# The parts of q and k: from SBUF straight into the stacks, instead of by a copy in DRAM

## What is computed

```
xn  = layernorm(x)
q,k,v = split(xn @ w_in.T + b_in)          # 16 heads of 8 features
scores = q @ k.T / sqrt(8), only where |i - j| <= 128
x1  = x + (xn + softmax(scores) @ v @ w_out.T + b_out) + int8_matmul(xn)
```

## Time and profile before

| | |
|---|---|
| median of 3 runs | 575.05 us (573.01 to 579.34) |
| the profiled execution | 578.81 us, its span 577.1 us |
| busy: PE, DVE, ACT, POOL | 87%, 76%, 59%, 53% of the span |
| mean granted clock of TensorE | 0.936 of full speed |
| DMA | 60.99 MB, 106 GB/s over the span |

### The profile page before, as it was taken

How to read it: one execution, slowest core, us unless ns; L and a number is a source line. 1 busy time by engine, 2 the same in 40 slices (tenths; PEclk the granted TensorE clock), 3 DMA queues, 4 the chain that set the end, 5 groups by cost and what they waited for, 6 DMA issues and landing times. The chain is left out here.

```text
span 577.1 us, 17179 instructions
## 1 busy us (share of the span) xinstructions
PE 499.8 (87%) x5731; PEld 320.9 (56%) x5731; DVE 440.9 (76%) x1888; ACT 341.7 (59%) x867; POOL 305.0 (53%) x361
## 2 busy tenths in 40 slices
PE   6278999999988998999989998988976899999990
PEld 5124444444443443444434446666654899999990
DVE  6698889798898896898886724899979567666662
ACT  2071777776766776577755675756556155555550
POOL 5680844816645556358110020557777567777662
PEclk9575999999999997999998999999998899999996
DMA  3856146274481653553810020711112233455534
GB/s 80 206 130 127 42 122 140 75 163 100 123 155 47 160 111 94 128 100 106 154 56 23 19 75 25 292 37 39 44 51 80 75 99 103 130 171 169 154 89 132
DMA packets 51383, 60.99 MB, mean 106 GB/s; under 512 B 10002, under 2 KB 42134, under 8 KB 49697
## 3 DMA queue, kind: packets, MB, share of 16 engines
q1 hardware_dynamic: 45824, 50.26, 36.0%
q0 software_dynamic: 4320, 8.47, 4.3%
q10 hardware_dynamic: 1152, 1.18, 0.7%
HBM read 31.68 MB, written 28.39 MB: 104 GB/s over the span
## 5 line engine op out<-in xcount | busy, mean ns | idle before, releaser
L704 DVE CUSTOM_DVE_ANT_0 A<-A,band 128x320 f32<-128x320 f32 (+2 forms) x512 | 213.6, 465 | 42.4 <-PE A L881 41.2
L881 PE MATMUL A<-Ks,Qs 48*64 48x320 bf16 (+2 forms) x1024 | 133.1, 310 | 22.5 <-DVE mneg L704 16.5
L911 PE MATMUL SB<-Qs,Ks 50*64 50x320 bf16 (+2 forms) x1024 | 133.8, 299 | 1.3 <-issue 0.6
L557 ACT ACTIVATE Pb<-SB 128x320 f32<-128x320 f32 x256 | 98.5, 441 | 42.2 <-PE SB L925 40.9
L881 PEld LDWEIGHTS A<-Ks,Qs 48*64 48x64 bf16 x1024 | 49.0, 107 | 128.1 <-DVE mneg L704 102.8
L1807 POOL DMA_INDIRECT results<-y,xt x71 | 73.9, 1041 | 36.1 <-issue 25.5
L554 ACT ACTIVATE Pb<-SB 128x384 f32<-128x384 f32 (+1 forms) x128 | 66.4, 545 | 43.8 <-PE SB L925 43.4
L938 PE MATMUL PV<-Pb,Va 128*32 128x320 f32 (+2 forms) x1024 | 87.5, 414 | 1.9 <-ACT Pb L554 1.6
L1258 POOL DMA_INDIRECT expert_rows<-pay,pos x64 | 61.9, 968 | 49.5 <-DVE pay L1441 30.9
L925 PE MATMUL SB<-ends,ident 64*64 64x128 bf16 x768 | 84.7, 222 | 0.0
L1928 PE MATMUL l_S<-xT,wt 128*128 128x128 f32 x568 | 75.1, 275 | 0.0
(11 more groups left out here) (264 smaller groups left out, 859.4 us busy)
## 6 DMA issues: line engine op xcount, KB each, us to landing
Qs<-parts_dram SPq DMA_DIRECT2D x14, 384.0 KB, 5.7
Ks<-parts_dram SPq DMA_DIRECT2D x14, 384.0 KB, 9.7
xt<-expert_rows SPq DMA_DIRECT2D x71, 65.0 KB, 1.9
yb<-results SPq DMA_DIRECT2D x7, 512.0 KB, 4.2
parts_dram<-qp SPq DMA_DIRECT2D x16, 192.0 KB, 2.8
parts_dram<-kp SPq DMA_DIRECT2D x14, 192.0 KB, 2.8
xb<-in_x SPq DMA_DIRECT2D x8, 256.0 KB, 3.0
parts_dram<-qp SPq DMA_DIRECT2D x16, 128.0 KB, 2.7
```

Of the source, the lines that this page charges most:

```text
L557: act.activation(Pb[:, group % 4, c, 0:w], bank[:, 0:w], ACT.Exp).then_inc(act_exp, 1)
L704: nc.vector.tensor_tensor_reduce(scores_of, scores_of, band[:, skip:skip + w], -1.0, 3e38, ALU.add, ALU.min, mneg[:, step % 2, col:col + 1 ...
L881: mm = nc.tensor.matmul(A[k % NA_BANKS][out:out + HP, 0:w], Qs[b % RING][rows, a, HP * sub:HP * sub + HP], Ks[b % RING][rows, a, lo:lo + w ...
L911: nc.tensor.matmul(out[r0:r0 + HP, at:at + w], Ks[b % RING][rows, a, HP * sub:HP * sub + HP], Qs[b % RING][rows, a, lo:lo + w], start=not ...
```

## The change

The terms are no longer stored to DRAM and read back. `stack_part` copies one part to one term's block of 8 rows: source 64 rows x 512 (64 KB), destination 8 rows x 8 x 512. That is 2 parities x 6 terms = 12 transfers for q and 12 for k in each batch, in place of 12 stores and 4 loads. The queue of SP changes with it: the transfers of q stay where the stores were, those of k go behind `place_max`. For batch 0 those of q are on SP's queue and those of k on ACT's. On DVE the fills of `Ks[0]` and `Va[0]` change places.

```diff
-QRUNS = ((0, 3, 0, 1), (3, 2, 1, 1), (5, 1, 2, 1))
-KRUNS = ((0, 3, 0, 3), (3, 2, 0, 2), (5, 1, 0, 1))
+QTERMS = ((0, 1, 2), (3, 4), (5,))
+KTERMS = ((0, 3, 5), (1, 4), (2,))
...
-    PARTS = 16 * 2 * len(QRUNS)
-    LOADS = 16 * 4
+    STACKED = 16 * 2 * NTERM
...
-    def store_run(engine, g, which, tile, run, done):
...
+    def stack_part(engine, g, which, part, done):
+        tile, stack, terms = ((qp, Qs, QTERMS), (kp, Ks, KTERMS))[which]
+        for n in terms[part]:
+            for par in range(2):
+                row = HP * par + HD * n
+                engine.dma_start(stack[g % RING][row:row + HD], tile[HP * par:HP * par + HP, part, :]).then_inc(done, 16)
...
-        def load(g):
...
-        def load_first():
...
+        def stack(g, which):
+            done, ready = ((dma_sq, pool_q3), (dma_sk, pool_k3))[which]
             if g >= RING:
                 sp.wait_ge(pe_B, STEP_FILLS * STEPS * (g - RING + 1))
+            sp.wait_ge(ready, g + 1 - which)
+            for part in range(3):
+                stack_part(sp, g, which, part, done)
...
-        store_first()
-        load_first()
+        stack_first()
         load_x(2)
-        store_parts(1, 0)
-        store_parts(1, 1)
+        stack(1, 0)
+        sp.wait_ge(act_fill, RING - 1)
+        stack(1, 1)
         place_max(0)
-        sp.wait_ge(act_fill, RING - 1)
-        load(1)
...
             if g < NB:
-                store_parts(g, 0)
-                store_parts(g, 1)
+                stack(g, 0)
...
             if b + 1 < NB:
                 place_max(STEPS * b + 2)
             if g < NB:
-                load(g)
+                stack(g, 1)
                 sp.wait_ge(pool_b2, g + 1)
...
         def evac_q1(g):
             if g > 0:
-                act.wait_ge(dma_pq, PARTS * g)
+                act.wait_ge(dma_sq, STACKED * g)
...
-        nc.vector.memset(Va[0][:], 0.0).then_inc(dve_const, 1)
+        fill(0)
...
-        fill(0)
+        nc.vector.memset(Va[0][:], 0.0).then_inc(dve_const, 1)
...
             if k == 0:
-                pe.wait_ge(dma_head, LOADS)
-            if k == UNITS:
-                pe.wait_ge(dma_stack, LOADS)
+                pe.wait_ge(dma_sq, STACKED)
+                pe.wait_ge(dma_sk, STACKED)
             if k > 0 and k % SLOTS == 0:
-                pe.wait_ge(dma_stack, LOADS * (b + 1))
+                pe.wait_ge(dma_sq, STACKED * (b + 1))
+                pe.wait_ge(dma_sk, STACKED * (b + 1))
```

More of the change, by code:

```diff
@@ L91, in layer0 @@
 def layer0(nc, ctx, x, w_inT, b_in, bv, w_outT, b_out, wqT, wscale, fbias, x1_dram, buf, later, follow):
-    parts_dram = nc.dram_tensor("parts_dram", [NB, 2, 2, NTERM, HP, T], BF16).ap()
     base_dram = nc.dram_tensor("base_dram", [NB, P, NT, P], F32).ap()
@@ L165, in layer0 @@
     misc16 = misc[:, 0:256].bitcast(BF16)
-    names = """dma_w dma_rows dma_x dma_base_r dma_base_w dma_pq dma_pk dma_head dma_stack dma_m dma_later pool_later
+    names = """dma_w dma_rows dma_x dma_base_r dma_base_w dma_sq dma_sk dma_m dma_later pool_later
     pool_const dve_fill act_fill dve_xn dve_k pool_rs pool_ve pool_xn pool_t1 pool_t2 pool_xq pool_b0 pool_b1 pool_b2
@@ L173, in layer0 @@
     s = {n: sem(n) for n in names}
-    (dma_w, dma_rows, dma_x, dma_base_r, dma_base_w, dma_pq, dma_pk, dma_head, dma_stack, dma_m, dma_later, pool_later,
+    (dma_w, dma_rows, dma_x, dma_base_r, dma_base_w, dma_sq, dma_sk, dma_m, dma_later, pool_later,
      pool_const, dve_fill, act_fill, dve_xn, dve_k, pool_rs, pool_ve, pool_xn, pool_t1, pool_t2, pool_xq, pool_b0, pool_b1, pool_b2,
@@ L231, in load_x, with stack_first @@
             sp.dma_start(xb[:], xv[g]).then_inc(dma_x, 16)
-        def store_first():
+        def stack_first():
             sp.wait_ge(act_q1, 1)
-            store_run(sp, 0, 0, qp, QRUNS[0], dma_pq)
+            stack_part(sp, 0, 0, 0, dma_sq)
             sp.wait_ge(pool_q2, 1)
-            store_run(sp, 0, 0, qp, QRUNS[1], dma_pq)
+            stack_part(sp, 0, 0, 1, dma_sq)
             sp.wait_ge(pool_q3, 1)
[L240 to L246, removed]
@@ L248, in load @@
-        def load(g):
-            pg = g % RING
+            stack_part(sp, 0, 0, 2, dma_sq)
+        def stack(g, which):
+            done, ready = ((dma_sq, pool_q3), (dma_sk, pool_k3))[which]
             if g >= RING:
                 sp.wait_ge(pe_B, STEP_FILLS * STEPS * (g - RING + 1))
[L253 to L259, removed]
@@ L528, in evac_k1 @@
         def evac_k1(g):
-            act.wait_ge(dma_pk, PARTS * g)
+            act.wait_ge(dma_sk, STACKED * g)
             act.activation(kp[:, 0, :], misc[:], ACT.Identity, bias=b_col[:, 1:2]).then_inc(act_k1, 1)
@@ L583, in _ @@
         evac_q1(0)
+        act.wait_ge(dve_fill, 1)
         act.wait_ge(dve_k, 2)
-        store_run(act, 0, 1, kp, KRUNS[2], dma_pk)
+        stack_part(act, 0, 1, 0, dma_sk)
         act.wait_ge(dve_k, 4)
-        store_run(act, 0, 1, kp, KRUNS[1], dma_pk)
+        stack_part(act, 0, 1, 1, dma_sk)
         act.wait_ge(dve_k, 5)
-        store_run(act, 0, 1, kp, KRUNS[0], dma_pk)
+        stack_part(act, 0, 1, 2, dma_sk)
         evac_xnT(1)
```

## The result

The changed kernel takes **590.37 us** (median of 4 runs, 586.30 to 592.96), the kernel before 574.03 us on the same chip (4 runs, 572.14 to 579.34). The ratio is 1.0263, its 95% interval 1.0166 to 1.036: slower by 16 us. The profiled execution took 588.51 us, with a span of 586.7. The direction was forecast, and so were the places; the size was not: 74 us were forecast.

The account below looks back on a forecast made before the run. PE and DVE bound the loop with loads barely hidden; the new transfers would not stay hidden. 13.5 + 11.6 + 42.6 + 9 - 2.8 = 74 us on the 575.05 median makes 649, called 650 us; range 576 to 712.

Parts of the forecast that it names:

- What bounds the kernel, and the question: Batch loop: PE and DVE bound it, stack loads are just hidden; the question is whether 24 new transfers stay hidden.
- The edits apart from the transfers: Queues and fills: swapped fills cost nothing, 12 issues take 7.3 us, base_r some 5 us later is hidden by slack.
- The price of a transfer: Time t one new transfer keeps its DMA engines from the next: 1.2 us, between 0.61 (issue) and 2.2 (prorated).
- Term 1, start: First piece on PE waits for all 24 transfers, landing at 42.9 instead of running at 29.43: 13.5 us late.
- Term 2, batch 1: `place_max` stands behind 24 transfers in SP's queue, so the scores that want it come 11.6 us late.
- Term 3, the loop: Six batches, each 1.9 us late for `place_max` behind q and 5.2 for k: 7.1 each, 42.6 us.
- Term 4, clock: Two stalls a batch make the granted clock fall from 1.00 to 0.50: 1.5 us a batch, 9 in all.
- Term 5, given back: PE's waits for the stack loads from DRAM go away: at most 2.8 us gained.
- Partly overlapped: Blocks in both halves or two queues written side by side, t 0.65 to 1.0: 576 to 600 us; chance 0.12.
- The engines keep up: SP's queue: transfers run fast enough to stay hidden, 572 to 575 us, or 568; chance 0.17.
- The prorated rival: Rate follows destination row count, 30 GB/s onto 8 rows, t = 2.2: some 835 us; chance 0.07.
- the working for t = 1.5: The same sum at 1.5 us a transfer: 20.7, 19.0, 6 x 14.3 and 9, less 2.8, giving 707 us.

Follow-up runs that it names:

- the start old: Changed kernel with batches 0 and 1 by the copy in DRAM as before, batches 2 to 7 by direct transfers: 579.46 us, ratio 1.0107 to the kernel before.
- the kernel with 16 transfers: Changed kernel with 16 instead of 12 transfers per set of parts, the four more writing rows that nothing reads: 620.98 us, the kernel before 573.16.
- the version with rows 6 apart: Changed kernel with stack rows interleaved, a transfer's 8 rows standing 6 apart: 570.62 us, ratio 0.9967 to the kernel before; repeated, 570.98 us, 0.9969.
- the two mixed kernels: Changed kernel with the DRAM copy kept for batches 0 and 1 only (579.46 us), or for batches 2 to 7 only (580.75 us, ratio 1.0146).
- the other kernel: Changed kernel with each 64 KB transfer spread over 16 neighbouring rows, four pairs in each, instead of 8 rows: 573.14 us, the kernel before 573.94.

## Why the prediction was wrong, point by point

- **What bounds the kernel, and the question: right.** The transfers were what counted, at the places named: the first piece, the first scores of batch 0, `mT` at a batch's first scores, k some 9 us into a batch.
- **The edits apart from the transfers: right.** The 12 issues of q take 7.8 to 8.5 us in the rows of SP's queue shown above, where 7.3 was forecast, and no new wait of PE is for base_r or a fill.
- **The price of a transfer: the step that failed.** It said "I take t = 1.2 us, the geometric middle of 0.61 and 2.2". Measured: 0.95 to 0.98 at 67 to 69 GB/s, 0.56 to 0.63 at 104 to 117. The 24 transfers at the start took 21.4 us from the first packet to the last, 0.89 each. The upper end, prorated from the 3.75 GB/s a row of the loads, belonged to another resource: the same stacks took 67 / 8 = 8.4 GB/s a row here, so it was not the count of rows in the destination that held the loads back; what did is not shown. The middle leaned on that end.
- **Term 1, start:** forecast 13.5 us, measured 5.8. With 0.89 in the same formula: 12.2 + 21.4 + 1.9 - 29.4 = 6.1. Formula right, size of t wrong. The earlier trace rows show 2.1 us as a whole and no latency of 1.9 by itself; here some 2.1 us lie outside the burst, 1.4 from the first issue to the first packet (11.65 to 13.08) and 0.7 from the last packet to the first piece (34.53 to 35.25).
- **Term 2, batch 1:** forecast 11.6, measured 9.9 - 5.8 = 4.1. With 0.89: 3.7 + 21.4 + 1.9 - 22.8 = 4.2. The same.
- **Term 3, the loop:** forecast 42.6, measured 6.7 with the start old, and 7.6 us of waits in the changed kernel (2.16 + 0.48 + 0.60 + 1.55 + 2.19 + 0.58 = 7.56). The size of t does most of it, as the term is steep in t: at 0.95 the same formula puts the parts of k at 22.5 + 24 x 0.95 + 1.9 - 46.1 = 1.1 us late in a batch, 6.6 in six, and `mT` not late at all (12 x 0.95 - 12.5 is below nothing). The places came out otherwise, so that 6.6 lies so near to 6.7 is partly luck. One t was used for every burst, so k was to be late in each batch; it was in two (1.55 and 2.19 us), those whose k ran at the slow price. `mT` was late by 0.5 to 2.2 us in the four others; in batch 1 the transfers of q went out at T + 24.0 (122.86 less 98.89) and not at T + 22.5, and for the other three the reason is open. In the kernel with 16 transfers, where every k of the loop ran fast, its wait fell away wholly.
- **Term 4, clock:** forecast 9. The granted clock does fall after the waits (0.50 in 99 to 103 us, at which TensorE runs at 1.2 GHz of its 2.4), but little time is left once the waits are taken off. Measured from the profile of the version with rows 6 apart, which has no wait for a transfer (span 568.2 us), it is 18.5 - 17.0 = 1.5 us for the changed kernel. For the kernel with 16 transfers (span 619.2) it is 51.0 - 41.4 = 9.6, so with waits as long as forecast 9 us could have been about right. In both, that remainder may hold other things than the clock, and no run sets the clock's part by itself.
- **Term 5, given back:** forecast 2.8; 1.7 us of PE's waits for loads in the same view went away. In the version with rows 6 apart, 2.2 us are gained in all.
- **The rivals.** "Partly overlapped", t from 0.65 to 1.0 and 576 to 600 us, is what happened by its t and its time; it had 0.12. So the measured time lies in the range 576 to 712 by this rival and not by the forecast. Its mechanism is not shown: some bursts run as if neighbouring transfers overlapped, but which blocks and halves follow each other changed nothing. "The engines keep up" had its price right: with rows 6 apart the time is 570.6 to 571.0, where 572 to 575, or 568, was forecast. The prorated rival (30 GB/s) is excluded by the 67 GB/s of the start.

Of the 74 us forecast, 16 came: by the two mixed kernels start and batch 1 gave 7.6 of 25.1 and the loop 6.7 of 42.6, what the clock took counted in, for which another 9 were forecast. In the working for t = 1.5 the term of batch 1 comes to 18.8 and not 19.0, on which nothing hangs.

## What to carry to other kernels

In this case the price of a transfer onto few rows followed how wide a stretch of rows it reached, not its bytes or the number of its rows: before a copy in DRAM is given up for many narrow transfers, see whether the order of the rows is free, since interleaving the blocks turned a loss of 2.6% into a gain of 0.3% here. Where an unknown price enters every term of a sum, look for the row that holds the same resource back, and don't take the middle of two ends of which one belongs to another resource. And a price measured in one burst need not hold in the next: the waits that rest on the second burst deserve a chance of their own.

## What the runs showed of the hardware

- Transfers onto 8 neighbouring rows from one queue do not have one price: those of k run at 117 and 104 GB/s for batches 2 and 3 and at 67 for batch 6, those of q at 69. The order of blocks and halves does not decide it.
- With the rows 6 apart the limit is probably the engines in use: 156 GB/s at a share of 0.53, while the pace of issue on the two queues (medians of 669 and 708 ns) would allow an estimated 190. No run shows it by itself. That a transfer onto 8 rows uses 8 of the 16 engines was left open in the prediction; it can be read now from the packets of ACT's queue at the start (12 to 36 and 12 to 35 us), with 12 transfers onto 8 rows each, and onto 16 rows each in the other kernel:

```profile
q10 hardware_dynamic: 864, 0.79, 23.1%
```

```profile
q10 hardware_dynamic: 960, 0.79, 26.8%
```

864 are 12 x (64 + 8), 960 are 12 x (64 + 16): beside 64 packets of 1 KB each transfer sends 8 small ones, or 16, and the busy share is 0.57 or 1.18 while it runs. That agrees with the Trainium skill (DMA: Bandwidth & Descriptors, Why a DMA increments its semaphore by 16 and not by 1), by which the slowest dimension sets how many engines take part and each of them ends with a write to the semaphore.
